# A one-core graph network: node stages unrolled over spans of four blocks, the row-of-ones product dropped, and the time embedding computed inside the message pass

## The reference, cut to what matters

```python
# L0, twice: edges, then nodes
x = relu(agg_f @ w_fwd[l] + agg_b @ w_bwd[l] + x @ w_loop[l])
# L1: edge messages, then nodes
agg = segment_sum(msg, dst) / (deg + 1e-8)
x = relu(concat([x, agg]) @ upd_w1 + upd_b1) @ upd_w2 + upd_b2
# L2: a time embedding of node_vec (one number per node), three GAT layers, an output product
emb = silu(pos_embed(node_vec) @ te_w1 + te_b1) @ te_w2 + te_b2
x = x @ init_w + init_b + emb
for layer in range(3):
    res = x @ adj_w + adj_b
    xw = x @ W;  al_s, al_d = terms(xw, a_src), terms(xw, a_dst)
    x = segment_softmax_sum(xw[src], al_s[src] + al_d[dst]) + bias + res
    x = silu(batch_norm(x))
x = x @ out_w + out_b
# L3: edge attention on K, V and Q = x @ W + b
```

## Time and profile before

| what | value |
|---|---|
| three runs | 9462.7, 9469.13, 9487.42 us; median 9469.13 |
| profiled execution | 9480.35 us; its span 9478.5 us, so 1.85 us lie outside the span |
| mean granted TensorE clock | 0.655 of full speed |
| PE, DVE, ACT, POOL busy | 69%, 48%, 21%, 64% of the span |
| the seven edge passes | 8375.4 us of the span |
| the thirteen node stages that the change touches | 873.9 us of the span |

### The profile page before, as it was taken

One profiled execution on the slowest core, in us unless ns is written; L12 is line 12 of the kernel. 1 busy time (PEld: TensorE's weight loads), 2 busy tenths in 40 slices (PEclk: granted clock), 3 DMA queues, 4 the chain that ended last, 5 costly groups with the idle time before them and its releaser, 6 DMA issues. The chain is left out here.

```text
span 9478.5 us, 139096 instructions
## 1 busy us (share of the span) xinstructions
PE 6510.8 (69%) x32379; PEld 5639.1 (59%) x32380; DVE 4520.1 (48%) x12932; ACT 2030.6 (21%) x5522; POOL 6088.3 (64%) x6396
## 2 busy tenths in 40 slices
PE   3556666666655556477877777777778888666766
PEld 3555556666544444346666646666667877566666
DVE  4444423333211111347777637777746666444444
ACT  2333321111122222212222212222122222211111
POOL 4777747777467777056666446666537777277776
PEclk7666555656577777567777767777755555566666
DMA  4555533333133333045555335554424444144443
GB/s 137 167 168 171 165 86 92 93 91 91 43 92 92 91 92 83 8 128 152 149 148 148 97 108 149 149 151 147 119 69 116 115 113 115 41 137 131 131 131 104
DMA packets 780185, 1092.58 MB, mean 115 GB/s; under 512 B 395392, under 2 KB 435008, under 8 KB 779728
## 3 DMA queue, kind: packets, MB, share of 16 engines
q1 hardware_dynamic: 546352, 588.70, 20.4%
q0 software_dynamic: 233760, 503.07, 20.1%
HBM read 1016.16 MB, written 75.04 MB: 115 GB/s over the span
## 5 line engine op out<-in xcount | busy, mean ns | idle before, releaser
L660 POOL DMA_INDIRECT gat_rows<-xw_table,gat_index x2736 | 2592.4, 948 | 1758.6 <-issue 1075.6
L1745 PE MATMUL bank<-gat_msg_s,gat_hot 128*128 128x264 f32 (+1 forms) x5472 | 1799.6, 497 | 27.2 <-DVE gat_msg_s L1660 26.5
L1745 PEld LDWEIGHTS bank<-gat_msg_s,gat_hot 128*128 128x128 f32 x5472 | 1322.7, 283 | 267.4 <-issue 32.0
L872 PE MATMUL bank<-gcn_rel,gcn_rhot 100*128 100x64 f32 x3648 | 763.3, 397 | 867.2 <-DVE gcn_rhot L827 867.0
L872 PEld LDWEIGHTS bank<-gcn_rel,gcn_rhot 100*128 100x128 f32 x3648 | 729.7, 306 | 911.3 <-issue 455.9
L660 POOL DMA_INDIRECT att_rows<-pre_table,att_index x912 | 862.8, 946 | 448.7 <-issue 276.0
L660 POOL DMA_INDIRECT msg_rows<-pre_table,msg_index x912 | 862.6, 946 | 412.7 <-issue 277.8
L660 POOL DMA_INDIRECT gcn_rows<-x_table,gcn_index x912 | 883.7, 969 | 361.5 <-issue 277.8
L660 POOL DMA_INDIRECT gcn_rows<-in_x,gcn_index x912 | 883.0, 968 | 333.9 <-issue 270.2
L1723 PEld LDWEIGHTS bank<-gat_ends_s,gat_hot 128*128 128x128 f32 x5472 | 966.7, 267 | 34.7 <-ACT gat_hot L698 2.9
L1723 PE MATMUL bank<-gat_ends_s,gat_hot 128*128 128x9 f32 x5472 | 916.8, 305 | 3.5 <-DVE gat_ends_s L1599 2.1
(11 more groups left out here) (300 smaller groups left out, 9118.8 us busy)
## 6 DMA issues: line engine op xcount, KB each, us to landing
gcn_ids<-rel_rows SPq DMA_DIRECT2D x228, 400.0 KB
gat_hot_half<-edge_hots SPq DMA_DIRECT2D x342, 256.0 KB
gat_dhot<-dst_hots SPq DMA_DIRECT2D x342, 256.0 KB
gcn_dst<-dst_rows SPq DMA_DIRECT2D x114, 512.0 KB, 6.7
gat_rows<-xw_table,gat_index POOLq DMA_INDIRECT x2736
edge_hots<-gcn_hot_half SPq DMA_DIRECT2D x114, 256.0 KB, 2.1
dst_hots<-gcn_dhot SPq DMA_DIRECT2D x114, 256.0 KB, 3.5
gcn_hot_half<-edge_hots SPq DMA_DIRECT2D x114, 256.0 KB
```

The lines of the kernel that those rows point to most:

```text
L660: pool.indirect_dma_start(self.rows[n.q][:, j, :], None, self.table, bass.IndirectOffsetOnAxis(ap=self.index[n.q][:, j:j + 1], axis=0))\
L872: ins = pe.matmul(rel_ps[q][:, j * DIM:(j + 1) * DIM], rhot[q][:, j * P:(j + 1) * P], rel[:, :], start=True, stop=True)
L1745: ins = pe.matmul(sum_ps[g][:, 0:wide], hot[n.q][:, g * GROUP + j, :], msg[q][:, g * GROUP + j, :], start=j == 0, stop=j == GROUP - 1)
```

## The change

What each part does:

- **Spans of four.** `SPANS` is seven spans: six of four blocks and one of one. In the node stages every loop over blocks is written out over spans. Tiles and banks come in pairs (`i % 2`), one copy out of PSUM takes up to 512 columns, and `in_turn` (in `message_nodes`: `staged`) writes the transposes of span i ahead of the products of span i-1. Transposes read the source tiles themselves, so the copies to `flat` go. A table is written by one DMA for each span.
- **No product with a row of ones.** `gat_tables` sets the columns of ones by a memset in `m.acc`; the weight tile holds 272 (144) columns without gaps, all eight banks are used, ACT copies the features out with a stride that skips those columns, and DVE copies the 16 term columns. The products read `cur` directly.
- **`gat_nodes`** multiplies by `adj_w` over 512 columns, makes the reciprocals ahead of the wait for its loads, and takes the statistics per span in the loop. Its Silu moves to the start of the next stage (`activate`, on ACT, in pieces of up to 512 columns).
- **Time embedding.** Its seven loads, angles (seven DVE operations on 512 columns instead of nine on 3200), Sin, two products and Silu go into `message_pass`, as parts with a count (TIMES = 7), one chunk of 512 nodes a step. They use one bank, taken from the pair that `turn` used. The result waits in `m.ft`, and `diffusion_embed` only adds x @ init_w.

```diff
--- before.py
+++ after.py
-ROUND = 5
+SPAN = 4
+SPANS = [(b, min(SPAN, NB - b)) for b in range(0, NB, SPAN)]
...
 def pipeline(eng, *parts, per_turn=RING):
...
+    head = -(-max(last, early) // per_turn) * per_turn
...
+            for lag, part, *count in parts:
+                if not count:
+                    part(Step(turn, (r - lag) // per_turn, (r - lag) % per_turn, per_turn))
...
+def in_turn(first, second):
+
+    for i in range(len(SPANS) + 1):
+        if i < len(SPANS):
+            first(i, *SPANS[i])
+        if i:
+            second(i - 1, *SPANS[i - 1])
...
 def compgcn_nodes(nc, m, a, layer, x, y):
...
+                def turn(i, b, size):
+                    if i >= 2:
+                        pe.wait_ge(agg_kept, i - 1)
+                        pe.wait_ge(x_kept, i - 1)
+                    for k in range(size):
+                        pe.transpose(agg_t[i % 2][:, k * P:(k + 1) * P], m.acc[:, b + k, 0:P], m.ident[:, :])
+                    for k in range(size):
+                        ins = pe.transpose(x_t[i % 2][0:DIM, k * P:(k + 1) * P], x[:, b + k, :], m.ident[:, :])
+                    ins.then_inc(turned, 1)
+
+                def products(i, b, size):
+                    pe.wait_ge(agg_kept, i + 1)
+                    pe.wait_ge(x_kept, i + 1)
+                    if i >= 2:
+                        pe.wait_ge(stored, i - 1)
+                    for k in range(size):
+                        out = res[i % 2][:, k * DIM:(k + 1) * DIM]
+                        pe.matmul(out, tall[i % 2][:, k * P:(k + 1) * P], w_agg[:, :], start=True, stop=False)
+                        ins = pe.matmul(out, tall_x[i % 2][:, k * P:(k + 1) * P], w_loop[:, :], start=False, stop=True)
+                    ins.then_inc(product, 1)
...
-                with pe.Fori(0, NB) as b:
-                    pe.wait_ge(staged, b * 2 + 2)
-                    pe.wait_ge(evacuated, b * 2 + 1)
-                    pe.transpose(agg_t[:, 0:P], flat[:, 0:P], m.ident[:, :])
-                    pe.transpose(x_t[0:DIM, 0:P], flat[:, P:3 * DIM], m.ident[:, :]).then_inc(turned, 1)
-                    pe.wait_ge(evacuated, b * 2 + 3)
-                    pe.wait_ge(stored, b + 1)
-                    pe.matmul(res[:, 0:DIM], tall[:, :], w_agg[:, :], start=True, stop=False)
-                    pe.matmul(res[:, 0:DIM], tall_x[:, :], w_loop[:, :], start=False, stop=True).then_inc(product, 1)
+                in_turn(turn, products)
...
-        turn_ps, edge_ps, sum_ps = m.ps[0:2], [m.ps[2:4], m.ps[4:6]], m.ps[6:8]
+        turn_ps, time_ps, edge_ps, sum_ps = m.ps[0], m.ps[1], [m.ps[2:4], m.ps[4:6]], m.ps[6:8]
...
+                def wave(n):
+                    part = chunk_of(n)
+                    act.wait_ge(angled, n.total(7, 7))
+                    act.activation(rnd[:, part], ang[:, part], ACT.Sin).then_inc(sined, 1)
...
+                def time_hidden(n):
+                    act.wait_ge(time_in, n.total(1, 1))
+                    act.activation(hid[:, 0:size_of(n)], time_ps[:, 0:size_of(n)], ACT.Silu, bias=b1[:, 0:1]).then_inc(time_hid, 1)
+
+                def time_keep(n):
+                    act.wait_ge(time_out, n.total(1, 1))
+                    act.activation(m.ft[:, 0, chunk_of(n)], time_ps[:, 0:size_of(n)], ACT.Identity, bias=b_in[:, 0:1])\
...
+                def angles(n):
...
+                    dve.wait_ge(node_in, 16 * 7)
+                    then(dve.tensor_scalar(x, x, freq[:, 0:1], freq[:, 1:2], ALU.mult, ALU.add))
+                    then(dve.tensor_scalar(turns, x, 1.0 / TURN, MAGIC, ALU.mult, ALU.add))
+                    then(dve.tensor_single_scalar(turns, turns, -MAGIC, ALU.add))
+                    for amount in (TURN_HI, TURN_MID, TURN_LO):
+                        then(dve.scalar_tensor_tensor(x, turns, -amount, x, ALU.mult, ALU.add))
+                    dve.tensor_scalar(x, x, 3.1415925, -3.1415925, ALU.min, ALU.max).then_inc(angled, 1)
...
+                def time_input(n):
...
+                    pe.matmul(time_ps[:, 0:size_of(n)], w1[:, :], rnd[:, chunk_of(n)], start=True, stop=True).then_inc(time_in, 1)
+
+                def time_output(n):
+                    pe.wait_ge(time_hid, n.total(1, 1))
+                    pe.matmul(time_ps[:, 0:size_of(n)], w2[:, :], hid[:, 0:size_of(n)], start=True, stop=True).then_inc(time_out, 1)
...
+                pe.wait_ge(node_in, 16 * 7)
+                pipeline(pe, (0, turn), (3, time_input, TIMES), (2, sums), (0, edge_products), (3, time_output, TIMES))
...
 def message_nodes(nc, m, a):
...
+                staged((0, turn), (1, turn_joined), (0, aggregate), (2, update), (1, hide))
...
 def diffusion_embed(nc, m, a, cur):
...
             def _(act):
-                act.wait_ge(step, 10)
-                act.activation(rnd[:, :], ang[:, :], ACT.Sin).then_inc(sined, 1)
-                with act.Fori(0, NB) as b:
-                    act.wait_ge(hidden_ps, b + 1)
-                    act.wait_ge(product, b + 1)
-                    act.activation(hid[:, :], h_ps[:, 0:P], ACT.Silu, bias=b1[:, 0:1]).then_inc(hidden, 1)
...
+def activate(act, m, layer, cur, counted):
+
+    ot = gat_shape(layer - 1)[1] // P
+
+    def part(i, b, size):
+        for o in range(ot):
+            tile = cur[:, o, b * P:(b + size) * P]
+            ins = act.activation(tile, tile, ACT.Silu, bias=m.shift[:, o:o + 1], scale=m.gain[:, o:o + 1])
+        ins.then_inc(counted, 1)
+    return part
...
 def gat_tables(nc, m, a, layer, cur):
...
-                dve.wait_ge(stored, NB + 2)
+                for b in range(NB):
+                    dve.wait_ge(kept, b + 1)
+                    dve.tensor_copy(m.acc[:, b, wide:both], m.ps[b % DEEP][:, width:width + 2 * HEADS]).then_inc(terms, 1)
...
+                def keep(b):
+                    act.wait_ge(product, b + 1)
+                    act.activation(by_head(m.acc[:, b, 0:wide])[:, :, 0:c], by_head(m.ps[b % DEEP][:, 0:width]), ACT.Copy)\
+                        .then_inc(kept, 1)
+
+                if layer:
+                    for i, span in enumerate(SPANS):
+                        activate(act, m, layer, cur, active)(i, *span)
+                for b in range(NB):
+                    keep(b)
 
...
-                def products(b, q):
-                    pe.wait_ge(stored, b + 1)
-                    pe.wait_ge(staged, b + 1)
-                    for k in range(kt):
-                        pe.matmul(o_ps[q][:, 0:both], flat[q][:, k, :], w[:, k, :], start=k == 0, stop=False)
-                    pe.matmul(o_ps[q][:, 0:both], m.ones[0:1, :], one[:, :], start=False, stop=True).then_inc(product, 1)
...
                 pe.wait_ge(folded, 1)
-                blocks_by_two(pe, products)
+                for i, (first, size) in enumerate(SPANS):
+                    if layer:
+                        pe.wait_ge(active, i + 1)
+                    for b in range(first, first + size):
+                        if b >= DEEP:
+                            pe.wait_ge(terms, b - DEEP + 1)
+                        for k in range(kt):
+                            ins = pe.matmul(m.ps[b % DEEP][:, 0:width + 2 * HEADS], cur[:, k, b * P:(b + 1) * P], w[:, k, :],
+                                            start=k == 0, stop=k == kt - 1)
+                        ins.then_inc(product, 1)
...
 def gat_nodes(nc, m, a, layer, cur, nxt):
...
+                def measure(i, b, size):
+                    dve.wait_ge(stored, i + 1)
+                    for o in range(ot):
+                        ins = dve.bn_stats(stats[:, o, i, :], nxt[:, o, b * P:min(N, (b + size) * P)])
...
+                dve.tensor_tensor(bias[:, :], bias[:, :], bias2[:, :], ALU.add).then_inc(biased, 1)
+                for i in range(1, len(SPANS)):
+                    divide(i, *SPANS[i])
+                    measure(i - 1, *SPANS[i - 1])
+                then(measure(len(SPANS) - 1, *SPANS[-1]))
                 for o in range(ot):
...
+                    if i >= 2:
+                        pe.wait_ge(stored, i - 1)
...
-                                            start=False, stop=k == kt - 1)
+                            pe.matmul(o_ps[i % 2][o][:, 0:size * P], adj[:, k, o * P:(o + 1) * P], cur[:, k, b * P:(b + size) * P],
+                                      start=k == 0, stop=False)
+                    pe.wait_ge(staged, i + 1)
+                    for o in range(ot):
+                        for j in range(size):
+                            ins = pe.matmul(o_ps[i % 2][o][:, j * P:(j + 1) * P], flat[i % 2][:, j, o * P:(o + 1) * P], m.ident[:, :],
+                                            start=False, stop=j == size - 1)
...
```

627 lines of the change are left out of this document (307 added, 320 removed).

## The result

Median 9027.52 us (four runs, 9025.46 to 9042.52) against 9468.91 before; the ratio is 0.9534, with a 95% interval of 0.9517 to 0.9551. The profiled execution took 9042.52 us with a span of 9040.4, 438.1 less than the span of before.

What follows compares the result with a forecast made beforehand. Gathers on POOL bound the passes, which stay; nothing overlaps the thirteen node stages (873.9 us), where engines take turns and PE's clock is mostly 0.50. Terms sum to 412.6 us saved, 9056.5 against the median: forecast 9057, range 8995 to 9100.

Steps and rivals of the forecast that it cites:

- Length after = edges + PE's stream: Node stages: length is first loads, last copies and table write plus PE's stream, if ACT and DVE keep below it.
- embed, the message pass: Embed falls from 135.4 to 23.6 us, saving 112; the message pass, taking the time embedding, loses 1 us.
- Table stages: gat_tab0 to gat_tab2: without one-row products the clock rises as in gat_nodes0; 145 us saved.
- rival A: The clock stays at 0.50 in the three table stages: 37.5 us more, 9094; chance 0.15.
- the 1.56 us: gat_tab0 to gat_tab2: cost per block of the one-row product with the change to it and back.
- gat_nodes, gat_out: Statistics under the products, Silu into the next stage, 4 us left behind the last product; 64.6 us saved.
- msg_nodes: PE's 49.2 us stays at clock 0.50, the stage falls from 86.1 to 59; 27 us saved, 37 at most.
- gcn_nodes: gcn_nodes0 and 1: 0.64 us a product, between 0.48 and 0.69, 45 us of stream each; 39 us saved.
- Rival B: The clock rises in the other dense stages too, from gcn_nodes to gat_out: 75 us less, 8982; chance 0.10.
- C: Message pass: the time embedding isn't hidden, 27 us more, 9084; chance 0.06.
- D: Node stages: spans don't overlap and PE still waits for ACT and DVE, 108 us, 9165; chance 0.05.
- E: Slower: the single bank for `turn` costs the message pass lastingly, 9490 at 3.8 us a step; chance 0.015.

Runs made afterwards that it cites:

- one-row run: Changed kernel with a one-row product of ones by zeros put back behind each block's products in gat_tab0 to gat_tab2; ratio 0.9681 to the kernel before.
- grouped run: Changed kernel with one-row products put back in gat_tab0 to gat_tab2, each span's four ahead of its feature products; ratio 0.9603 to the kernel before.
- series run: Changed kernel without overlap of spans in gcn_nodes, the projections, msg_nodes and embed, each span finished before the next; ratio 0.9621 to the kernel before.

## Why the prediction was right, and where it was off

- **What bounds it:** right. The sum of the passes moved by 2.9 us, and the gain stands in the thirteen stages, 442.1 us of a span that got 438.1 shorter.
- **"Length after = edges + PE's stream":** right as a form. PE's idle time in the stages was to fall from 326 to the 110 of edges; it is 110.4.
- **embed, the message pass:** right, 112 and -1 against 113.1 and -0.5. By experiment the pass pays 1 to 4 us.
- **Table stages:** the number held (145 and 148), and the clock went where I chose; rival A (clock 0.50, 9094) didn't come. The step "what tells them apart is the one-row products, which use one row of the array" was right only in part: grouped, the same one-row products let the clock rise to 0.64 to 0.79, so their order counts too. Whether by the changes of rows or by leaving the 128-row products in one stretch isn't settled. The price of the 1.56 us was read rightly: 0.9 for the product's columns at clock 0.50, and 0.6 for the change and back. In the one-row run a product starts every 1.20 us at that clock, and in the grouped run four of a kind take 3.92 us with one change, which makes 0.91 for the columns and 0.29 for a change.
- **gat_nodes, gat_out:** 64.6 and 61.7; the tail behind the last product was put at 4 us and is 4.
- **msg_nodes, the term most mis-sized:** "PE's 49.2 stays at clock 0.50". It is 35.14 at 0.71. I had read the clock of before as a property of the stage; the series run shows that it came with the pauses. "The 37 us of idle are the most it could give" was wrong for the same reason: it gave 41.7, since PE's own 49.2 shrank.
- **gcn_nodes:** "I stay near the upper one, 0.64" a product, and 45 us of stream a stage; the streams measured 38.4 and 40.9. At clock 0.50 a product takes 0.62 us, of which 0.19 is the change of rows (forecast 0.16) and 0.43 the base (forecast 0.48). The rest is transposes, 0.21 us from start to start where 0.26 was taken, and some of the clock in gcn_nodes0 (0.54). How much of the clock a run gets varies with nothing changed: the two stages took 41.3 to 46.5 and 37.1 to 45.5 us in the eight runs with this code.
- **The total:** with msg_nodes and gcn_nodes forecast 26 us too low together and the other terms right within 4, 9027.5 came close to the low end of the forecast's own bounds (9025 to 9090). No two large errors cancelled.
- **Rival B** (clock up in all other dense stages, 8982) came true in one stage, and that one is half of the deviation. What kept it from coming true in gcn_nodes, the projections and embed is shown as far as padding shows it: with their 64-row products padded they reach 0.74 to 0.86, and the kernel 8960.54 us. For gat_out it isn't: its products have 128 rows, PE ran them 10.93 us without a pause, and the clock was 0.50 in every run of the changed form. The Trainium skill (TensorE: Matmul & The Clock Gate, "What's actually happening") ties the clock to how busy the PE is. Embed after the change, PE without a pause at 0.50, and its padded form at 0.77 do not agree with a reading of "busy" as "has an instruction running".
- **Rivals C, D, E:** out. C by the run without the embedding (1 to 4 us). D by PE's idle time of 110.4 us; the series run shows what it would have cost, 70 to 82 us.

## What to carry to other kernels

In this kernel a product with few rows isn't a cheap product: it takes as long as its columns say, and a change of the row count costs extra (0.19 us between 128 and 64, some 0.3 each way between 128 and 1, in fp32 at clock 0.50). Streams in which short products and 128-row ones alternate had little of the clock (0.50 in the table stages, 0.50 to 0.65 in gcn_nodes). So look for short row counts in any stretch where PE is busy without a pause at 0.50, and try padding them with zeros; in the table stages that alone, in the old loop, gave 115 of the 148 us. Overlap paid twice in msg_nodes, where it closed the last pauses, once by the wait and once by the clock. A function on ACT inside a loop, behind another function's table, can load its table each turn: in embed before the change Silu did, 25 x 1.28 us. Do all of one function and then all of the other, as the new form does with two loads; whether the loop or the order of functions caused the 25 loads wasn't tried apart.
